# Recommender kernel: gathers in sample order, pair products spread over the layers, one store, layer 4 behind the pairs

## The reference

```python
fm = emb_table[arange(26)[None, :], cat_idx]            # 512 x 26 rows of 128 floats
h = relu(dense_x @ Wd1 + bd1)                           # 13 -> 512
h = relu(h @ Wd2 + bd2)                                 # 512 -> 256
dense = relu(h @ Wdf + bdf)                             # 256 -> 128
Z = concat([fm, dense[:, None, :]], axis=1)             # 512 x 27 x 128
S = einsum('bie,bje->bij', Z, Z)                        # every pair of the 27 vectors of a sample
x = concat([S[:, iu, ju], dense], axis=-1)              # 351 pairs + 128
x = relu(x @ Wt1 + bt1)                                 # -> 1024
x = relu(x @ Wt2 + bt2)                                 # -> 1024
x = relu(x @ Wt3 + bt3)                                 # -> 512
x = relu(x @ Wt4 + bt4)                                 # -> 256
return sigmoid(x @ Wo + bo)                             # 512 x 1, float32
```

## Time and profile before

| | |
|---|---|
| median of 3 runs | 210.7 us (208.46 to 212.02) |
| the profiled execution | 208.52 us |
| its span, first to last instruction | 205.6 us |
| mean granted TensorE clock | 0.918 of full speed |
| PE busy | 163.3 us (79%) |
| POOL busy | 104.0 us (51%) |
| DVE busy | 63.8 us (31%) |
| ACT busy | 49.6 us (24%) |

### The profile page before, as it was taken

One profiled execution on the slowest core, in us unless ns is written; L12 is line 12 of the kernel. 1 busy time (PEld: TensorE's weight loads), 2 busy tenths in 40 slices (PEclk: granted clock), 3 DMA queues, 4 the chain that ended last, 5 costly groups with the idle time before them and its releaser, 6 DMA issues.

```text
span 205.6 us, 3860 instructions
## 1 busy us (share of the span) xinstructions
PE 163.3 (79%) x1744; PEld 122.5 (60%) x1744; DVE 63.8 (31%) x90; ACT 49.6 (24%) x82; POOL 104.0 (51%) x111
## 2 busy tenths in 40 slices
PE   2999992034379999896999989899998689998820
PEld 1334431024369788674988867698886579886510
DVE  3044408051154522315351321535241153122110
ACT  2455785040052211111421011231201111111100
POOL 3777878777777777777777777770000000000000
PEclk9999999555558999999999999999999999999985
DMA  3989987689543332444337444441000000000000
GB/s 103 323 233 299 285 198 181 132 253 364 177 55 51 49 54 51 51 58 56 57 51 46 58 57 54 56 60 14 0 0 0 3 6 0 0 0 0 0 0 0
DMA packets 8890, 17.66 MB, mean 86 GB/s; under 512 B 3249, under 2 KB 4529, under 8 KB 8746
## 3 DMA queue, kind: packets, MB, share of 16 engines
q0 software_dynamic: 3328, 6.82, 22.8%
q1 hardware_dynamic: 5546, 10.60, 15.3%
HBM read 17.41 MB, written 0.00 MB: 85 GB/s over the span
## 4 chain that ended last, share of the span: by engine, by line
PE 61%; DMA 19%; DVE 7%; issue 5%; ACT 3%; SPq 1%; DVEq 0%
PE mp L388 22%; DMA w<-in_wt 18%; PE mp L408 12%; PE tp L359 12%; PE gp L336 6%; PE gp L326 4%; DVE xb L608 3%; PE tp L368 3%; PE tp L348 1%; ACT a2h L505 1%; DMA idx<-in_cat_idx 1%; DVE raw L636 1%; PE mp L424 1%; ACT xt L497 1%; DVE xp L610 1%
## 5 line engine op out<-in xcount | busy, mean ns | idle before, releaser
L276 POOL DMA_INDIRECT rows<-in_emb,row_of x104 | 103.1, 992 | 34.0 <-issue 30.5
L326 PE MATMUL gp<-ident,rows 128*128 128x128 f32 x104 | 16.9, 288 | 12.0 <-DMA rows<-in_emb,row_of 12.0
L359 PE MATMUL tp<-xt,w 117*128 117x128 f32 x192 | 25.2, 287 | 1.5 <-ACT xt L497 1.2
L388 PE MATMUL mp<-w2h,a1h 128*128 128x512 f32 x64 | 26.1, 409 | 0.0
L388 PE MATMUL mp<-w2l,a1h 128*128 128x512 f32 x64 | 25.6, 399 | 0.0
L388 PE MATMUL mp<-w2h,a1l 128*128 128x512 f32 x64 | 25.6, 399 | 0.0
L359 PEld LDWEIGHTS tp<-xt,w 117*128 117x128 f32 x192 | 23.8, 201 | 2.4 <-ACT xt L497 1.5
L326 PEld LDWEIGHTS gp<-ident,rows 128*128 128x128 f32 x104 | 13.4, 149 | 15.9 <-DMA rows<-in_emb,row_of 13.3
L336 PE MATMUL gp<-zt 128*32 128x27 f32 x1024 | 14.2, 205 | 9.9 <-issue 7.9
L336 PEld LDWEIGHTS gp<-zt 128*32 128x32 f32 x1024 | 12.3, 120 | 13.0 <-issue 12.8
L486 ACT COPY zt<-gp 128x512 f32<-128x512 f32 (+1 forms) x16 | 8.6, 535 | 34.7 <-PE gp L326 34.7
(11 more groups left out here) (58 smaller groups left out, 156.9 us busy)
## 6 DMA issues: line engine op xcount, KB each, us to landing
w<-in_wt SPq DMA_DIRECT2D x13, 512.0 KB, 5.7
rows<-in_emb,row_of POOLq DMA_INDIRECT x104, 3.5
w<-in_wt SPq DMA_DIRECT2D x3, 468.0 KB
bc<-in_rows SPq DMA_DIRECT2D x1, 1024.0 KB
wd_sb<-in_wd SPq DMA_DIRECT2D x1, 512.0 KB, 3.4
w1d<-in_wt SPq DMA_DIRECT2D x1, 512.0 KB, 5.9
wdf_sb<-in_wdf SPq DMA_DIRECT2D x1, 128.0 KB, 4.1
out<-probs SPq DMA_DIRECT2D x4, 0.5 KB, 7.7
```

The source lines that it names most:

```text
L276: pool.indirect_dma_start(out=rows[:, n % RING, :], out_offset=None, in_=emb.rearrange("c v e -> (c v) e"), in_offset=bass.IndirectOffsetO ...
L326: last = pe.transpose(gp[:, g % 4, n * P:(n + 1) * P], rows[:, (N_CAT * t + f0 + n) % RING, :], ident[:])
L359: last = pe.matmul(tp[:, m // 4, (m % 4) * P:(m % 4 + 1) * P], w1[0:PC, k, m * P:(m + 1) * P], xt[0:PC, k, :], start=(k == 0), stop=(k == ...
L388: last = pe.matmul(mp[:, h, :], a[:, k, :], w[:, k, cols], start=(k == 0 and part == 0), stop=(k == M1 - 1 and part == 2))
```

## The change

- **Gathers.** Gather `n` of a tile brings 128 consecutive rows of the tile in the order sample, feature: row `n * 128 + p` of 128 x 26. The host lays `cat_idx` out so that each gather's indices are one column; the base of each table is computed by four small DVE instructions from a 13-column pattern. The number of gathers, their size and POOL's loop over them are as before; the ring has 40 slots.
- **Bank copies.** A transposed bank now holds 512 consecutive columns, some 19 samples of 26. `bank_pieces` copies it to `zt` in two or three instructions (whole samples, and the part of a sample at either end). Banks are two of their own (`ft`), and ACT and DVE take them in turn over all tiles.
- **Grams.** `grams(t, b)` multiplies the groups of samples that are complete after bank `b`, four or five groups (three in the last). The table `STEPS` lays transposes and grams of the next tile between the products of layers 1 to 3; the last grams are ahead of product 15 of layer 3. `turn(t, 1)` is ahead of product 6 (it was 12).
- **A tile's end.** PE: `turn(t, 2)`, `transpose_pairs(t + 1)`, `layer_4(t)`. DVE: the first block transpose, `layer_3_sum(t)`, the second block transpose, the copy of pairs. ACT: `pairs_in`, `relu_3`, `pairs_out`.
- **Loads.** SP issues `bc` and the four pieces of `w3` only after tile 0's last gather has landed; their splitting moves into layer 2 of tile 0.
- **Output.** The four columns of logits are transposed by PE to four rows, one sigmoid, one store of four rows of 512 bytes.

```diff
+STEPS = {
+    2: [("t", 0)], 5: [("g", 0)], 6: [("t", 1)], AT_2 + 4: [("g", 1)], AT_2 + 10: [("t", 2)], AT_2 + 18: [("g", 2)],
+    AT_2 + 27: [("t", 3)], AT_2 + 36: [("g", 3)], AT_2 + 42: [("t", 4)], AT_3 + 2: [("g", 4)], AT_3 + 5: [("t", 5)],
+    AT_3 + 10: [("t", 6)], AT_3 + 13: [("g", 5)], AT_3 + 15: [("g", 6)],
+}
+TURN_2 = (PRODUCTS_2 // 2 + 6, 6)
+SPLIT_3 = (10, 20, 34, 44)
...
+        ft = pb("ft", [P, 2, 512])
+        gp = pb("gp", [P, 2, 512])
...
+        def bank_pieces(n):
+            b = n % NB
+            at, end = Z_BANKS[b][0] * P, (Z_BANKS[b][0] + Z_BANKS[b][1]) * P
+            first, last = -(-at // N_CAT), end // N_CAT
+            samples = zt[:].rearrange("p g q f -> p (g q) f")
+            bank = ft[:, n % 2, :]
+            pieces = [(samples[:, first:last, 0:N_CAT], bank[:, first * N_CAT - at:last * N_CAT - at].rearrange("p (s f) -> p s f", f=N_CAT))]
+            if at % N_CAT:
+                pieces.append((samples[:, first - 1, at % N_CAT:N_CAT], bank[:, 0:N_CAT - at % N_CAT]))
+            if end % N_CAT:
+                pieces.append((samples[:, last, 0:end % N_CAT], bank[:, last * N_CAT - at:end - at]))
+            return pieces
...
-            for n in range(M1, SPLIT_LOADS):
-                sp.wait_ge(w1_in[2] if n < M1 + 2 else w_in[n - 2], 16)
+            sp.wait_ge(gathered[0][NB - 1], 16 * Z_BANKS[NB - 1][1])
+            sp.dma_start(bc[:], ...).then_inc(rows_sem, 16)
+            for n in range(M1, SPLITS):
+                if n >= M1 + 1:
+                    at_least(sp, rows_sem if n == M1 + 1 else w_in[n - 2], 16)
                 load_to_split(n)
...
-            for t in range(TILES):
-                sp.wait_ge(probs_ready, t + 1)
-                sp.dma_start(out[t * P:(t + 1) * P, :], probs[:, t:t + 1]).then_inc(out_done, 16)
+            sp.wait_ge(probs_ready, 1)
+            sp.dma_start(out.rearrange("(t p) o -> t (p o)", p=P), probs[:]).then_inc(out_done, 16)
...
+            def grams(t, b):
+                n = NB * t + b
+                if b == 0:
+                    pe.wait_ge(zt_dense, t + 1)
                     at_least(pe, xb_ready, 2 * t)
+                pe.wait_ge(zt_dve if n % 2 else zt_act, n // 2 + 1)
+                if b > 0:
+                    pe.wait_ge(zt_act if n % 2 else zt_dve, (n - 1) // 2 + 1)
+                for g in range(READY[b], READY[b + 1]):
+                    r, k = divmod(g, HALF_G)
+                    for q in range(Q):
+                        last = pe.matmul(gp[32 * q:32 * (q + 1), r, NZ * k:NZ * (k + 1)], zt[:, g, q, :], zt[:, g, q, 0:NZ],
+                                         start=True, stop=True)
...
-            for g in range(3, NG):
-                transpose_features(0, g)
-            for g in range(GROUPS):
-                gram(0, g)
+            grams(0, 0)
+            grams(0, 1)
+            for b in range(3, NB):
+                transpose_bank(0, b)
+                grams(0, b - 1)
+            grams(0, NB - 1)
...
-                for g in range(done, done + TURN_AFTER):
-                    gram(t + 1, g)
-                turn(t, 2)
-                for g in range(done + TURN_AFTER, GROUPS):
-                    gram(t + 1, g)
-                layer_4(t)
-                transpose_pairs(t + 1)
+                    turn(t, 2)
+                    transpose_pairs(t + 1)
+                    layer_4(t)
...
             layer_4(t)
+            pe.wait_ge(logits_ready, TILES)
+            pe.transpose(gp[0:TILES, 0, 0:P], logits[:], ident[:]).then_inc(row_ready, 1)
...
-                for x, n in ((xb[:, 0:NZ, :], NZ), (xb[:, NZ:NZ + HALF, :], HALF)):
-                    ve.transpose(x, sums(n)).then_inc(xb_ready, 1)
+                ve.transpose(xb[:, 0:NZ, :], sums(NZ)).then_inc(xb_ready, 1)
+                if before is not None:
+                    layer_3_sum(before)
+                ve.transpose(xb[:, NZ:NZ + HALF, :], sums(HALF)).then_inc(xb_ready, 1)
```

More of the change, by code:

```diff
@@ L150, in build @@
         idx_step = sem("idx_step")
-        gathered = [[sem(f"gathered{p}_{g}") for g in range(NG)] for p in range(2)]
+        gathered = [[sem(f"gathered{p}_{b}") for b in range(NB)] for p in range(2)]
         bot_ready = sem("bot_ready")
@@ L160, in build @@
         zt_dve = sem("zt_dve")
+        zt_dense = sem("zt_dense")
         gram_ready = sem("gram_ready")
@@ L194, in pairs_of, with steps, pairs_bank @@
             return bass.AP(tensor=flat.tensor, offset=flat.offset + 33 * i0 + 32, ap=[list(flat.ap[0]), [33, n], [32, HALF]])
[L196 to L209, removed]
+        def bank_pieces(n):
[10 more added lines that the diff above has]
+            return pieces
+        def steps(t, place):
+            return STEPS.get(place, ()) if t < TILES - 1 else ()
+        def pairs_bank(t):
+            return ft[0:PC, NB * (t + 1) % 2, 0:PAIR_CHUNKS * P]
         def split_weights(n):
@@ L269, in _ @@
             pool.wait_ge(idx_step, 4)
[L270 to L279, removed]
+            for n in range(GATHERS):
+                t, f = divmod(n, N_CAT)
+                if n >= RING:
+                    before, was = divmod(n - RING, N_CAT)
+                    pool.wait_ge(ft_ready, NB * before + was // ZG + 1)
+                pool.indirect_dma_start(
+                    out=rows[:, n % RING, :], out_offset=None, in_=emb.rearrange("c v e -> (c v) e"),
+                    in_offset=bass.IndirectOffsetOnAxis(ap=row_of[:, n:n + 1].bitcast(U32), axis=0),
+                ).then_inc(gathered[t % 2][f // ZG], 16)
         @block.tensor
@@ L329, in gram, with transpose_bank @@
[L329 to L337, removed]
-                    last.then_inc(gram_ready, 1)
+            def transpose_bank(t, b):
+                n = NB * t + b
+                first, count = Z_BANKS[b]
+                pe.wait_ge(gathered[t % 2][b], 16 * count * (t // 2 + 1))
+                at_least(pe, zt_dve if n % 2 else zt_act, n // 2)
+                for k in range(count):
+                    last = pe.transpose(ft[:, n % 2, k * P:(k + 1) * P], rows[:, (N_CAT * t + first + k) % RING, :], ident[:])
+                last.then_inc(ft_ready, 1)
@@ L340, in transpose_pairs, with next_tile @@
+            def next_tile(t, place):
+                for step, b in steps(t, place):
+                    if step == "t":
+                        transpose_bank(t + 1, b)
+                    else:
+                        grams(t + 1, b)
             def transpose_pairs(t):
@@ L367, in turn @@
                 for c in range(4):
-                    last = pe.transpose(tp[:, h % 2, c * P:(c + 1) * P], raw[:, h % 2, c * P:(c + 1) * P], ident[:])
+                    last = pe.transpose(tp[:, min(h, 1), c * P:(c + 1) * P], raw[:, h % 2, c * P:(c + 1) * P], ident[:])
                 last.then_inc(turned, 1)
@@ L428, in _ @@
             pe.wait_ge(ident_made, 2)
-            for g in range(2):
-                transpose_features(0, g)
+            transpose_bank(0, 0)
+            transpose_bank(0, 1)
             pe.wait_ge(w1d_in, 16)
@@ L554, in _ @@
                 for n in range(PRODUCTS_2):
-                    for g in FEATURES_2[t].get(n, ()):
-                        if g % 2 == 0:
-                            features(t + 1, g)
-                    if t >= 1 and n == 1:
-                        sigmoid(t - 1)
-                    if n == TURN_2:
+                    next_tile(t, AT_2 + n)
+                    if t == 0 and n in SPLIT_3:
+                        split_hi(M1 + SPLIT_3.index(n))
+                    if n == TURN_2[0]:
                         layer_2_hi(t, 0)
@@ L584, in _ @@
+            ve.wait_ge(base_step, 2)
+            ve.scalar_tensor_tensor(out=base[:, 0, :], in0=of_26[:, 1, :], scalar=float(-N_CAT), in1=place[:], op0=ALU.mult,
+                                    op1=ALU.add).then_inc(base_step, 1)
+            ve.wait_ge(base_step, 3)
+            ve.tensor_scalar(base[:, 1, :], base[:, 0, :], float(VOCAB), None, ALU.mult).then_inc(base_step, 1)
             ve.wait_ge(idx_in, 16)
@@ L673, in _ @@
                         layer_2_sum(t, 0)
[L674 to L677 removed]
+                    next_tile(t, AT_2 + n)
+                    if t == 0 and n - 2 in SPLIT_3:
+                        split_lo(M1 + SPLIT_3.index(n - 2))
+                    if n == TURN_2[0]:
                         layer_2_lo(t, 0)
```

240 lines of the change are left out of this document (107 added, 133 removed).

## The result

The changed kernel takes 186.06 us (median of 4 runs, 185.39 to 186.99) against 210.77 us (median of 4, 208.46 to 212.02): a ratio of 0.886, 95% interval 0.878 to 0.895. The forecast was 189.0, the sum of its steps 188.1, against the profiled execution of before, 208.52 us; the profiled one of after took 186.12. Ratios are of undisturbed executions alone, so one can differ a little from the ratio of two medians.

What follows compares the result with a forecast made beforehand. It took the start as bound by something other than PE, four tiles by PE, the end by nobody. Terms -10.8 - 4.5 - 5.1 = -20.4 took 208.52 to 188.1 us; forecast 189.0, range 185 to 196.5.

Steps and rivals of the forecast that it cites:

- the start: Up to layer 1 of tile 0: faster last gather, fewer grams behind it; -10.8 us, bounds -7 and -11.5.
- the end: After the last layers: added transpose +0.4, store of four rows -5.5; together -5.1 us, bounds -5.5 and +0.4.
- the loop: Layer 3 to the end: holes -3.9, tile's end +1.8, turn -2.7, bank copies +0.3; -4.5 us, bounds -6.5 and -1.
- Gathers as nearly the bound for tile 0: Tile 1's last gather would land under 1 us before PE asks for it; cost 0, bound +1.5 us.
- The rival that PE stays cold: Around the start, the clock returns only at the old time despite the earlier layer 1; +5 us, 194; chance 0.08.
- Holes: Holes among the grams between tiles would vanish once grams are spread among products; gain 3.9 us in the loop.
- Turn ahead of product 6: In layer 3, six products would cover PE's 0.69 us wait for ACT's relu in four tiles; -2.7 us.
- A tile's end and the grams: Layer 3 to next layer 1: 4.2 us plus 3.8 grams plus 0.3 against 7.7; +1.8 us over three tiles.
- The copy of bank 1 on ACT ahead of the relu: Ahead of `layer_1_hi`, PE may wait 0.2 us where ACT copies bank 1; +0.3 us taken for the kernel.
- The store: At the end, four rows of 512 bytes would be waited for about 1.7 us instead of 7.2; -5.5 us.
- Holes and the fetch of instructions: Holes among the grams were read as PE running out of instructions where a hundred and more small matmuls follow each other.

Runs made afterwards that it cites:

- run 4: The kernel before with only the indices changed, so gathers bring rows in the order sample, feature; 206.37 us, ratio 0.996.
- run 3: The changed kernel with the loads of `w3` issued behind `w1` as before, not held back until tile 0's last gather; 187.98 us.
- runs 7 and 8: First the changed kernel with tile 0's grams in one lump, 262.89 us; then the kernel before with `w3` and bias loads held back, 269.87 us; kernel before beside them 269.52.
- run 12: Changed kernel: layer 3's sum behind block transposes, pairs before turn, layer 4 inside next layer 1, layer 1's relu and low part before bank 1's copy; 181.59 us.
- run 2: The changed kernel with all 256 gram records of the next tile in one lump ahead of product 15 of layer 3; 195.16 us, ratio 0.939.
- Run 5: The changed kernel with `turn(t, 1)` ahead of product 12 of layer 3 again; 266.0 us, on a chip where the kernel before took 269.52.
- run 1: The changed kernel with the old end: a sigmoid and a store of 128 4-byte values per tile, no transpose of logits; 193.11 us, ratio 0.930.
- runs 5 to 7: Changed kernel with, in order: second turn ahead of product 12, layer 4 ahead of pairs, tile 0's grams in one lump; 266.0, 266.84, 262.89 us (kernel before 269.52).

## Why the prediction was right, by its steps

The starts of layer 1 came at 47.76, 85.13, 119.63 and 154.62, where about 48, 85, 119.5 and 154 had been forecast. The profiled execution is 2.0 us under the 188.1 of the steps: 0.6 from the start, 0.9 from the end and 1.1 from outside the span, less 0.6 that the loop gained too little.

**The start: forecast -10.8, measured -11.4.** The gather went out at 38.91, 0.55 earlier than before (its indices landed 0.3 sooner, the rest lies in POOL's own issues), and landed after 3.41, within the bounds. The forecast put the faster landing down to the loads, and for this gather that holds: it took 5.0 us before, 4.9 in run 4 (new order of rows, loads in flight), 4.80 in run 3 (the same in the changed kernel) and 3.41 with the loads held back. So the loads are worth 1.4 us and the order of the rows 0.1 or 0.2; for gathers with nothing beside them the order is worth 0.8 (run 4), which the forecast did not have. Behind the landing the forecast had 24 gram records (0.4) and a bare bank copy (0.6). In fact 64 records stand there (1.13), and the copy is hidden beneath the first 40 of them. With the transposes that makes 1.9 us for the 1.5 forecast, and it came so near by luck. How much of the remaining gain was the lump and how much the hole isn't separated: the bound is arithmetic (4.03 of hole, 1.60 of waiting for DVE's copy, 192 records at 16.5 ns = 3.2), and runs 7 and 8 did not answer.

**Gathers as nearly the bound for tile 0: right.** The forecast had a cover of under 1 us at the last gather of tile 1. It was issued at 72.29 (72.2 forecast), 3.8 us ahead of its transposes; with the 2.5 that gathers take there, an estimate since its own landing isn't recorded, the cover was 1.3. In run 12 it went out 0.5 later and PE came 1.2 earlier, and the cover was used up.

**The clock.** It came back in the window 52 to 53 us (0.92), 4.3 us behind the start of layer 1, as it had some 4 behind it before. The rival that PE stays cold until the old time is out.

**Holes: right, and shown.** Forecast -3.9 in the loop; all are gone, and run 2 brings them back by density alone. The forecast did not have it that they can take the clock with them.

**Turn ahead of product 6: mis-sized.** The term was -2.7, from a wait of 0.69 in four tiles. Run 5 measures 1.2 in the last tile and 1.0 in tile 2; if tiles 0 and 1 are like tile 2, that is -4.2. The named wait was only a part of the cost, and the low part's lateness lay inside PE's busy time.

**A tile's end and the grams: mis-sized the other way.** The boundary came as forecast, 4.17 for 4.2. The grams did not. Tile 1's layers take 30.40 us against 23.03 in tile 3, so 7.37 more. Of that, 2.86 are the 26 transposes and 0.24 is what the turn gains less among grams, which leaves 4.3 us a tile where the term had 3.8. Two things are in it. The rows that the term cites (240 records in 3.43 us) give 14.3 ns a record, not 13.5. And the chain shows what a switch costs: a gram group of 40 records takes 0.48, a little less than its 0.54 at 13.5 ns, and the six products behind it take 1.59 instead of the 1.40 they take elsewhere, so together some 0.13 more, not 0.06. Over three boundaries the part costs 3 x (4.17 + 4.3 + 0.3 - 7.7) = +3.2, not +1.8. The copy of bank 1 on ACT ahead of the relu cost 0.45 in each of two tiles, +0.9 for +0.3; run 12 shows the cause by taking it away.

Together: -3.9 - 4.2 + 3.2 + 0.9 = -4.0, measured -3.9. The forecast's -4.5 was near it by luck: an error of 1.5 us in the turn stood against errors of 1.4 and 0.6 the other way. That the new sum fits to 0.1 is partly luck too, since it still holds two errors of about 1 us. The three boundaries before, without their holes, were 7.6, 7.6 and 6.7 us, not 7.7 each, so 1.1 less was to be gained. And layer 1 of the three later tiles follows upon layer 4 now, which nobody had counted: in tile 3 it takes 5.36 instead of 5.62, and 0.8 for the three by estimate from that one.

**The end: forecast -5.1, measured -6.0.** The transpose, its handshakes and the longer sigmoid cost 0.4, as taken. The store was waited for 0.9 us, not 1.7. The width of the store as the cause is shown by run 1; why values of 4 bytes land late is not. The Trainium skill (DMA: Bandwidth & Descriptors, Specifications) says that below 512 bytes a transfer does a read-modify-write. That points the right way, though no run here shows that this is the mechanism.

**Outside the span,** 1.1 us more was gained, which no step had. It belongs to the change, at least in part: every execution of the changed kernel and of its variants has 1.8 or 1.9 us there, while those of the kernel before, with runs 4 and 8, have 1.8 to 3.1, with medians of 2.1 to 2.7 on the three chips. What in the change does it is open. It isn't the store, because run 1 with the old stores has 1.8 too.

**Holes and the fetch of instructions.** The Trainium skill (Runtime: NRT & Kernel Launch, Instruction fetch mechanics) would hide the fetch of 256-instruction blocks. If the holes are that fetch, the traces agree while products of 0.23 us run and disagree for small matmuls in a row: 14 packets, no hole, in the changed kernel; 14 packets and four holes of 0.96 to 2.52 us in run 2. That PE lacks instructions in a hole is my reading of the place of the packets; density as the cause is shown, the fetch is argued.

## What to carry to other kernels

Small matmuls should stand between long ones, in groups of some tens of records: a lump of 256 leaves holes that no semaphore explains and that can halve PE's clock, though each switch costs 0.1 to 0.2 us. The price of a late operand isn't the wait that the profile names: look also for a run of products that takes longer than the same number elsewhere. And store results as rows: one small PE transpose at the end bought 6 us.

## What the hardware showed that was not expected

- Gathers of 128 rows of 512 bytes land in a median of 2.6 us when their rows come from 26 tables in turn, and in 3.4 us when they come from one (run 4 and the kernel before, same stretch, same number of packets; each packet keeps its engine busy for 16 x 27.4 / 3328 = 0.13 us instead of 0.23, 27.4 us being 13.5% of run 4's span). Which property of the addresses does it was not tried. Beside the loads of `w3` little of it is left for gather 25: 4.9 against 5.0.
- A store of 128 values of 4 bytes takes 6.6 to 8.3 us to land (run 1), and gathers that fly beside it land late: up to 8.0 us in run 1, where the changed kernel's longest from 100 to 130 us was 3.2. It shows only with the rows in the new order. Beside the same store run 4 has 6.1 us at most, the kernel before 3.7, of the landings that are recorded.
- Behind holes of 0.96 and 2.12 us, with 126 small matmul records between, the granted clock fell from 1.00 to 0.50 and came back some 10 us later; behind one of 2.52 us it fell for 3 us. Behind one of 1.38 us it stayed (all in run 2).
- On one chip all five kernels tried took 60 to 80 us longer, with PE, ACT and DVE idle for nothing that the traces record: 41 to 54 us of it on PE ahead of small matmuls in runs 5 to 7, and single waits of ACT of up to 19.2 us in run 8. From tile 2's layer 2 on, runs 5 to 7 went at the usual rate. A comparison across chips would have called any of these kernels 60 us slower.
